# Local attention layers: the mask written by ScalarE, and three reorderings on VectorE, GpSimd and ScalarE

## The reference, cut to what matters

```
q = l2norm(q) * qs;  k = l2norm(k) * ksc           # 16 heads of 64
q, k = rotary(q) * scale, rotary(k) / scale
sim = einsum(q, [previous window, own window of k]) * 8    # windows of 32
attn = softmax(where(mask, -max, sim))
x = concat(attn @ v) @ Wo + x                        # tokens shifted before
x = ffn(layernorm(shift(x))) + x                     # gelu(gate) * a
```

## Time and profile before

| | before |
|---|---|
| median of 3 runs | 3906.66 us (3903.13 to 3911.06) |
| profiled execution, its own time | 3922.45 us |
| its span, first to last instruction | 3920.6 us |
| busy PE / PEld / DVE | 3244.6 / 2478.3 / 2604.8 us |
| busy ACT / POOL | 1958.9 / 1731.4 us |
| mean granted TensorE clock | 0.896 |

### The profile page before, as it was taken

The page is one execution under the profiler, slowest core; times in us unless marked ns, Lnnn a source line. Parts: engine busy times, 40 slices in busy tenths (PEclk is TensorE's granted clock), DMA queues, the critical chain, the costliest instruction groups (busy, mean ns, idle before and its releaser), DMA issues. The chain is left out here.

```text
span 3920.6 us, 124571 instructions
## 1 busy us (share of the span) xinstructions
PE 3244.6 (83%) x53825; PEld 2478.3 (63%) x53825; DVE 2604.8 (66%) x4478; ACT 1958.9 (50%) x3747; POOL 1731.4 (44%) x1651
## 2 busy tenths in 40 slices
PE   6665948999999999999999997599898886876557
PEld 2223537788888778878887886367676665522235
DVE  6996457777777777677767774655565543599813
ACT  5542226666666666666666664234444433255323
POOL 1662026565565556555555552422222221056542
PEclk8997969999999999999999998768888876889878
DMA  1000011111111101101100000000000000000111
GB/s 43 1 1 19 0 41 49 38 29 44 38 29 44 38 27 46 38 27 44 38 27 27 27 27 14 7 6 7 7 7 7 7 5 7 8 1 1 65 58 47
DMA packets 72473, 96.86 MB, mean 25 GB/s; under 512 B 14678, under 2 KB 48244, under 8 KB 70788
## 3 DMA queue, kind: packets, MB, share of 16 engines
q1 hardware_dynamic: 69668, 84.74, 7.3%
q0 software_dynamic: 2272, 4.27, 0.3%
HBM read 35.60 MB, written 8.40 MB: 11 GB/s over the span
## 5 line engine op out<-in xcount | busy, mean ns | idle before, releaser
L2208 POOL TENSOR_TENSOR local_rot<-local_term 128x512 f32<-128x512 f32 x384 | 479.3, 1269 | 651.3 <-DVE local_term L2554 651.3
L2554 DVE TENSOR_TENSOR local_term<-bank,local_table 128x512 f32<-128x512 f32 x768 | 486.0, 683 | 261.5 <-ACT local_sq L2432 259.9
L2214 POOL TENSOR_TENSOR local_rot<-local_rot,local_inv 128x512 f32<-128x512 f32 x384 | 396.7, 1054 | 107.4 <-ACT local_inv L2443 89.2
L278 POOL TENSOR_TENSOR mamba_hc<-mamba_state,mamba_c_all 128x512 f32<-128x512 f32 x256 | 325.9, 1295 | 256.5 <-DVE mamba_state L502 249.1
L2242 PE MATMUL bank<-local_w_layer,local_xs 128*128 128x256 f32 x1536 | 393.4, 400 | 7.9 <-ACT local_xs L2426 3.4
L2242 PEld LDWEIGHTS bank<-local_w_layer,local_xs 128*128 128x128 f32 x1536 | 282.3, 194 | 49.2 <-issue 4.2
L339 PE MATMUL bank<-mamba_hc,ident 128*128 128x512 f32 x512 | 263.9, 641 | 24.0 <-DVEq L511 18.3
L2432 ACT ACTIVATE local_sq<-bank 128x512 f32<-128x512 f32 x384 | 222.5, 592 | 48.3 <-PE bank L2242 47.0
L2464 ACT ACTIVATE local_attn<-last_banks 128x512 f32<-128x512 f32 x192 | 115.0, 599 | 262.1 <-PE last_banks L2305 262.1
L2566 DVE TENSOR_REDUCE local_sums_q<-local_sq 128x8 f32<-128x512 f32 x384 | 243.2, 674 | 0.0
L2284 PEld LDWEIGHTS bank<-local_k_rot,local_q_rot 64*32 64x32 f32 x12288 | 184.9, 109 | 71.5 <-issue 71.5
(11 more groups left out here) (456 smaller groups left out, 8006.7 us busy)
## 6 DMA issues: line engine op xcount, KB each, us to landing
local_v_moved<-local_v_at SPq DMA_DIRECT2D x192, 198.0 KB
local_w_layer<-a_w_layer_dram SPq DMA_DIRECT2D x6, 1536.0 KB, 7.1
local_v_moved<-local_v_at SPq DMA_DIRECT2D x192, 33.0 KB
routed_w<-f_w_dram SPq DMA_DIRECT2D x3, 2048.0 KB, 16.1
local_w_o<-a_w_o_dram SPq DMA_DIRECT2D x6, 512.0 KB, 3.8
rows_dram<-fresh SPq DMA_DIRECT2D x1, 2574.0 KB, 12.6
routed_x_in<-rows_dram SPq DMA_DIRECT2D x13, 198.0 KB, 4.6
routed_y_in<-y_dram SPq DMA_DIRECT2D x8, 256.0 KB, 4.9
```

Source lines behind the costliest of these rows:

```text
L278: ins = pool.tensor_tensor(hc[:, n % 2, h, :], state[:, n % 2, h, :], c_all[:, n % 2, :], ALU.mult)
L2208: pool.tensor_tensor(rot[:, s % 2, :, f, :], here[:, :, f, :], there[:, :, 1 - f, :], ALU.add).then_inc(summed, 1)
L2214: pool.tensor_tensor(one, one, spread(inv[:, s % 2, heads], E), ALU.mult).then_inc(normalized, 1)
L2554: dve.tensor_tensor(term[:, which, b, :], g.bank[b][:, :], table[:, which, :, :].rearrange("p n c -> p (n c)"), ALU.mult).then_inc(roped, 1)
```

## The change

Four edits. (1) The mask matmul is left out for all slots but the first; instead ScalarE copies the mask into the score bank for slot s+1, right behind the exponent of slot s (`open_scores`), and TensorE's scores wait for that copy (`opened`). (2) VectorE sums and inverts the softmax weights (`invert_weight`) before the sums of squares, not after. (3) GpSimd divides the probabilities between the sums and the scaling of the rotated heads, not behind both. (4) ScalarE's place "middle" (residual copy at position 2, inverse deviation at position 4) stands right behind `copy_probs`, ahead of the copies of queries, keys and values.

```
             def add_turned(s):
                 pool.wait_ge(roped, s * 4 + 8)
                 here, there = by_half(term[:, 0, :, :]), by_half(term[:, 1, :, :])
                 for f in range(2):
                     pool.tensor_tensor(rot[:, s % 2, :, f, :], here[:, :, f, :], there[:, :, 1 - f, :], ALU.add).then_inc(summed, 1)
+                if s >= 2:
+                    normalize_probs(s - 2)
                 pool.wait_ge(inv_ready, s + 1)
...
                 if s + 2 < SLOTS:
                     add_turned(s + 2)
-                normalize_probs(s)
+                else:
+                    normalize_probs(s)
...
             def score(s):
-                pe.wait_ge(z_ready, s + 1)
-                pe.matmul(S_BANK[:, :], ident_b[:, :], mask[:, :, :].rearrange("p x k -> p (x k)"),
-                          start=True, stop=True, skip_group_check=True)
+                if s:
+                    pe.wait_ge(opened, s)
+                else:
+                    pe.matmul(S_BANK[:, :], ident_b[:, :], mask[:, :, :].rearrange("p x k -> p (x k)"),
+                              start=True, stop=True, skip_group_check=True)
...
+            def open_scores(s):
+                act.wait_ge(z_ready, s + 1)
+                act.activation(S_BANK[:, :], mask[:, :, :].rearrange("p x k -> p (x k)"), ACT.Copy).then_inc(opened, 1)
...
                 exponents(s)
+                if s + 1 < SLOTS:
+                    open_scores(s + 1)
                 if s + 2 < SLOTS:
                     square(s + 2, 0)
                     square(s + 2, 1)
                 beside(s, "second")
                 if s:
                     copy_probs(s - 1)
+                beside(s, "middle")
                 if s + 1 < SLOTS:
                     copy_queries(s + 1)
                     copy_keys(s + 1)
                 if s + 2 < SLOTS:
                     copy_values(s + 2)
-                beside(s, "middle")
...
+                invert_weight(s)
+                if ahead:
                     add_squares(s + 2)
-                invert_weight(s)
                 beside(s, "last")
```

More of the change, by code:

```diff
@@ L2086, in local_stack @@
         s_ready, z_ready, e_ready = sem("s_ready"), sem("z_ready"), sem("e_ready")
-        over_ready, p_normed = sem("over_ready"), sem("p_normed")
+        over_ready, p_normed, opened = sem("over_ready"), sem("p_normed"), sem("opened")
         pt_ready, pt_copied, o_ready, o_copied, wo_ready = (
@@ L2202, in _, with normalize_probs @@
             pool.sem_inc(made, 1)
+            def normalize_probs(s):
+                pool.wait_ge(over_ready, s + 1)
+                rows = z[:, s % 2, :].rearrange("p (x k) -> p x k", k=2 * W)
+                pool.tensor_tensor(rows, rows, spread(over[:, s % 2, :], 2 * W), ALU.mult).then_inc(p_normed, 1)
             def add_turned(s):
@@ L2215, in add_turned @@
                                        ALU.mult).then_inc(normalized, 1)
[L2216 to L2219, removed]
             pool.sem_inc(summed, 2)
```

## The result

The change makes the kernel slower: 3933.33 us (median of 20 runs, 3915.51 to 3945.77) against 3912.57 of before in the same series (20 runs), a ratio of 1.0041, 95% interval 1.0025 to 1.0058. The forecast was 3900, with a range up to 3928. The profiled execution has a span of 3936.5 against 3920.6, so 15.9 more; its mean granted clock is 0.892 against 0.896.

What follows compares the result with a forecast made beforehand. VectorE's chain with ScalarE was taken as the bound: 20 x 75.71 + 10.2 + 3 = 1527.4, a gain of 10.5; +3.6 outside, net -6.9, 3915.5 profiled, so a forecast of 3900 us; range 3876 to 3928.

Steps and rivals of the forecast that it cites:

- The chain: Steps between VectorE's row maxima, summed over one stall-free period of eight slots: 75.25 us before, 75.71 forecast; chance 0.50.
- position 4: Slot with the layer norm: +0.53 for the mask, -1.02 as the norm no longer waits, together -0.49 us.
- The mask copy's 0.53: ScalarE's 128x512 copy between exponent and first square: step of 0.53 us, bounds 0.49 and 0.60.
- Position 3: Slot where the mask adds 0.53 and the exponent, queued behind the later inversion of norms, 0.66: +1.19 us.
- the wait of position 2: TensorE's wait for the residual copies, 37.4 us in 20 cases; taken as gone, with the low clock behind it.
- TensorE's other stalls: TensorE stalls apart from the residual-copy wait, over 20 periods: hidden behind VectorE, all but an estimated 3 us.
- the excess: Time of 20 whole periods over 20 quiet ones: 32.9 us before, forecast at 13.2.
- what lies outside the 20 periods: Four periods without residual copies to move: lose about 0.9 us each, +3.6.
- The table products: Five products of 2.03 us each on VectorE's chain: half their time counted before, now in full, 10.2.
- the clock falls in new places: Rival: TensorE waits for rotated heads, 1.6 us at position 0, and its clock falls: 3928; chance 0.15.
- ScalarE's copy is dearer: Rival: the mask copy's step is 0.60 us, with 0.53 in full at position 1: +22, 3922; chance 0.12.
- TensorE is the bound after all: Rival: mask matmuls and waits for division and residuals all come back: 168 us, 3739, half of it 3823; chance 0.17.

Runs made afterwards that it cites:

- residual_copies_alone: Kernel before with only the residual copies and inverse deviation moved ahead of the copies of queries, keys and values (edit 4): 3862.32 us, ratio 0.9856.
- mask_on_tensor: Changed kernel with the mask matmul back on TensorE in every slot (edit 1 undone), edits 2 to 4 kept: 3844.57 us, ratio 0.9823.
- old_order_at_four: mask_on_tensor with edits 2 and 3 undone at position 4 alone: 3858.16 us, ratio 0.9862.
- mask_behind_squares: Changed kernel with ScalarE's mask copy moved behind the two squares: 3870.18 us, ratio 0.9892.
- mask_on_both: mask_behind_squares with TensorE's mask matmul added again on top of the copy: 3857.39 us, ratio 0.9863.
- tensor_mask_idle: mask_on_tensor with two semaphore increments without work more per slot in TensorE's program, ahead of the mask matmul: 3866.58 us, ratio 0.9895.
- behind_squares_shift: mask_behind_squares with 128 instructions without work once, ahead of TensorE's first slot: 3903.66 us, ratio 0.9974.

## Why the prediction was wrong

**The chain was right in the main.** A quiet period of 75.71 was forecast, and 75.76 came; that the sum is so close is partly luck, as position 4 (0.39 too long) makes up for the others. The mask copy's 0.53 measured 0.52. By the Trainium skill (ScalarE: Activation LUTs, section "What ACT_TABLE_LOAD costs") the estimate was 0.52, and the trace agrees. Positions 0, 1, 2 and 5 to 7 are within 0.08. Position 3 came out 0.21 shorter; there the exponent starts 2.09 behind the maximum, not 2.22. That edits 2 to 4 only pay for the mask copy was right too, and the experiments show it apart: edits 4, 3 and 2 alone bring -54.9, -20.0 and nothing, together -67 in one kernel, and the copy +88.8.

**The step that failed** is "With the wait of position 2 gone I take the clock's part as gone, and TensorE's other stalls as hidden behind VectorE, all but an estimated 3." Its first half held: the low clock behind the wait of position 2, eight of the nine low stretches of before, is gone. The second half failed. After the change TensorE pauses in the weighing for 0.8 us or more 21 times in the 20 periods instead of three times, for 0.8 to 2.2 us each, and 13 of the 14 stretches at the lower level (47.8 us, before 44.4) begin within 1.6 us of such a pause's end. The places depend on the count of instructions in TensorE's program; six of the pauses stand at position 1, where TensorE sets the end and nothing hides them. residual_copies_alone shows the same exchange: the wait is gone and the excess still 33.4. The two parts of that sum measured 31.9 together with the tables, where 13.2 had stood. This is 18.7 of the 22.8 by which the span missed (+15.9 instead of -6.9). The chain is 1.0 of it, and what lies outside the 20 periods another 3.1 (6.7 instead of 3.6): the four periods there take 14.3 more, and the layers outside the stack, which the change leaves alone, some 7.7 less.

**Two terms were off in opposite ways.** The table products were to count in full, 10.2; position 6 takes 8.77 to 8.79 instead of 8.68 in four of the five periods that have one (9.68 in the fifth), about 0.1 each, as VectorE makes the table in its wait for ScalarE's square. With it the stalls were missed by more than the sum shows: about 31 instead of 3.

At position 4 the layer norm no longer waits, as forecast, but it is slower. Groups by line and form of the kernel before (count, then busy us and mean ns, then idle time ahead):

```profile
L2585 DVE TENSOR_SCALAR local_h<-local_h,local_vecs 128x512 f32<-128x512 f32 x24 | 27.7, 1155 | 0.9
L2583 DVE TENSOR_TENSOR local_h<-local_xc,local_rstd 128x512 f32<-128x512 f32 x24 | 16.6, 692 | 31.4 <-ACT local_rstd L2478 31.4
```

The same groups after the change:

```profile
L2595 DVE TENSOR_TENSOR local_h<-local_xc,local_rstd 128x512 f32<-128x512 f32 x24 | 28.8, 1200 | 4.3 <-ACT local_rstd L2488 4.2
L2597 DVE TENSOR_SCALAR local_h<-local_h,local_vecs 128x512 f32<-128x512 f32 x24 | 26.9, 1123 | 0.9
```

And in residual_copies_alone:

```profile
L2583 DVE TENSOR_TENSOR local_h<-local_xc,local_rstd 128x512 f32<-128x512 f32 x24 | 28.0, 1165 | 4.2 <-ACT local_rstd L2478 4.2
L2585 DVE TENSOR_SCALAR local_h<-local_h,local_vecs 128x512 f32<-128x512 f32 x24 | 13.1, 546 | 0.9
```

The first multiplication takes 692 ns where GpSimd stands idle at its start (before, where GpSimd waited for the inverse norms) and 1165 to 1206 where one of GpSimd's sums is under way. The second takes 546 where GpSimd pauses at its start, and 1123 to 1155 where it works. The trace shows the manner of it: in mask_on_tensor, after, residual_copies_alone and old_order_at_four the first multiplication ends 0.55 behind the end of the GpSimd instruction that was under way at its start, in all 92 cases, and the second, where it meets one, 0.28 behind, in all 92 cases of before, after, mask_on_tensor and old_order_at_four. So VectorE waits for that instruction to end. 0.5 of the 1.02 that position 4 was to save went to this contention. The Trainium skill (SBUF — State Buffer, section "Who interferes with whom") says that a VectorE instruction with two inputs from SBUF gets in the way of GpSimd's reads, and that the form with a scalar can do so too; the trace agrees with 0.69 against 1.20 and 0.55 against 1.12. This rests on rows of different kernels; no experiment turned it alone.

**The rivals.** The time lies nearest to "the clock falls in new places", 3928. Its time is nearly right and its place wrong: TensorE did wait for the rotated heads (59.4 in 69), but position 0 was as reckoned, and the clock fell behind the pauses in the weighing. "ScalarE's copy is dearer" is out (0.52), and so is "TensorE is the bound after all": less work on it gave 0.16 a period (mask_behind_squares against mask_on_tensor), and mask_on_tensor, with more, is fastest. Finally, the forecast was missed by 33.3, the span by 22.8. The median of before was 3912.57 in 20 runs, 5.9 above that of the three which the forecast started from, and the profiled execution after the change stood 4.9 over its median, not 15.8. From 3912.57 the upper end of the range would have been 3934, so the time falls outside it by less than that shift.

**What stays open:** why some packets of instructions come in time and others too late. That a burst of small matmuls outruns them is my reading and was not shown. Why the clock falls behind some pauses and not behind others, and so why mask_on_both has six low stretches and mask_on_tensor two, is open too.

## What to carry to other kernels

Ask of a moved operation whether it lands in the loop that sets the pace: 0.2 us taken off TensorE cost 0.52 or more in six of eight slots, because the copy stood ahead of the squares; one place further back it cost nothing in the quiet period. Time a bundle's edits one by one, since three that gain or do nothing can hide one that loses. And forecast that what a stretch takes beyond its quiet period stays: here the event behind it did go away, and another took its place. A change of instruction count moves such pauses, and by itself it shifted a kernel here by 22 us (mask_on_tensor to tensor_mask_idle), as much as this whole change did.

## What the runs showed of the hardware

- TensorE pauses, for 0.8 to 2.2 us and at times up to 4.1, inside bursts of small matmuls, at places that hang on the number of instructions ahead in its program; 128 instructions more moved the pattern by 11 periods.
- In all 266 pauses of the 14 traces a 16 KB packet of the instruction queue lands 1.20 to 1.64 us before the pause ends.
- A pause of 1.35 us was followed by eight matmuls in 3.68 instead of 2.12, part of them at the lower level of the clock (0.90 granted over 17.7 us).
- 128 instructions that only raise a semaphore took TensorE 18.5 us, 0.14 each (behind_squares_shift).
- VectorE's 128x512 product of two SBUF tiles took 0.69 with GpSimd idle at its start, and ended 0.55 behind GpSimd's instruction where one was under way (1.17 to 1.21 in all).
